# Order of PE's work in a chunk of the convolution part: taps of block 1 and transform 3

## The reference

```python
# layer 0: linear attention
q = elu(to_heads(rope(Wq x + bq)) * scale) + 1;  k = elu(to_heads(rope(Wk x + bk))) + 1;  v = to_heads(Wv x + bv)
out = (q @ (k^T v)) / (q . sum(k) + 1e-6);       layer = Wfc out + bfc
# layer 1: the convolution part
t = einsum('bchw,oc->bohw', x, w_in)             # 384 -> 384
tf = rfft2 of t in 8x8 patches * fft_filter;     t = irfft2(tf)
t = depthwise 3x3 convolution of t with w_dw     # padding SAME
x1, x2 = t[:, :192], t[:, 192:]
layer = einsum('bchw,oc->bohw', gelu(x1) * x2, w_out)
```

## Time and profile before

| | us |
|---|---|
| median of 3 runs | 3960.15 |
| lowest, highest | 3959.14, 3964.23 |
| the profiled execution, its own time | 3959.47 |
| its span, first to last instruction | 3957.6 |
| PE busy | 3490.4 (88%) |
| DVE busy | 3178.0 (80%) |
| POOL busy | 1795.7 (45%) |
| ACT busy | 1629.6 (41%) |

### The profile page before, as it was taken

The page is one execution under the profiler, slowest core; times in us unless marked ns, Lnnn a source line. Parts: engine busy times, 40 slices in busy tenths (PEclk is TensorE's granted clock), DMA queues, the critical chain, the costliest instruction groups (busy, mean ns, idle before and its releaser), DMA issues.

```text
span 3957.6 us, 61233 instructions
## 1 busy us (share of the span) xinstructions
PE 3490.4 (88%) x17808; PEld 3021.8 (76%) x17808; DVE 3178.0 (80%) x4879; ACT 1629.6 (41%) x2781; POOL 1795.7 (45%) x1114
## 2 busy tenths in 40 slices
PE   5988989889898898988989889897889979899798
PEld 4976779767796677966779677896768957699676
DVE  7976979769797697976879768897688976888777
ACT  2423634246342463425633255332553316533164
POOL 2543535435354353553435534454344544444443
PEclk9998989999998999999989899898999989999899
DMA  5113322133212332123321233213332133221322
GB/s 201 64 56 136 119 77 69 64 120 120 89 56 72 121 119 81 57 87 120 112 76 61 88 112 112 89 48 103 109 107 81 48 114 109 96 81 56 128 88 104
DMA packets 186274, 371.18 MB, mean 94 GB/s; under 512 B 7947, under 2 KB 9011, under 8 KB 185779
## 3 DMA queue, kind: packets, MB, share of 16 engines
q1 hardware_dynamic: 186034, 368.26, 27.2%
HBM read 267.56 MB, written 100.66 MB: 93 GB/s over the span
## 4 chain that ended last, share of the span: by engine, by line
issue 33%; PE 30%; POOL 18%; DVE 14%; ACT 3%; DMA 1%; POOLq 1%; DVEq 1%; SPq 0%; ACTq 0%
POOL t L445 9%; POOL x_lo L438 6%; PE bank L1234 5%; PE bank L1200 3%; DVE bank L942 3%; PE bank L1075 3%; PE bank L1076 3%; PE bank L1080 3%; POOL qn L482 3%; PE bank L1207 3%; DVE nrm L850 2%; DVE qt_lo L865 2%; PE bank L1154 2%; DVE xr L878 2%; DVE bn_x L911 2%
## 5 line engine op out<-in xcount | busy, mean ns | idle before, releaser
L445 POOL TENSOR_TENSOR t<-t 128x768 f32<-128x768 f32 x256 | 535.4, 2092 | 726.4 <-DVE t L786 726.4
L1076 PE MATMUL bank<-w_lo,x_hi 128*128 128x384 f32 x2322 | 792.7, 341 | 34.1 <-issue 34.1
L1075 PE MATMUL bank<-w_hi,x_hi 128*128 128x384 f32 x2322 | 789.7, 340 | 4.0 <-ACT x_hi L537 4.0
L438 POOL TENSOR_TENSOR x_lo<-xa,x_hi 128x512 fp32r<-128x512 f32 x363 | 495.9, 1382 | 592.0 <-ACT x_hi L537 592.0
L942 DVE SCALAR_TENSOR_TENSOR bank<-big,wdw,bank 128x512 f32<-128x512 f32 x960 | 685.7, 750 | 94.5 <-PE bank L1234 91.3
L506 POOL TENSOR_TENSOR prod<-prod 128x512 f32<-128x512 f32 x320 | 409.1, 1278 | 489.1 <-ACT prod L629 479.0
L542 ACT ACTIVATE t<-t 128x768 f32<-128x768 f32 x256 | 217.1, 848 | 929.1 <-POOL t L445 929.1
L1080 PE MATMUL bank<-w_hi,x_lo 128*128 128x384 f32 x2322 | 542.3, 342 | 0.5 <-POOL x_lo L438 0.5
L796 DVE SCALAR_TENSOR_TENSOR kt<-t 128x384 f32<-128x384 f32 x256 | 533.6, 2084 | 0.0
L1076 PEld LDWEIGHTS bank<-w_lo,x_hi 128*128 128x128 f32 x2322 | 441.4, 190 | 36.3 <-issue 36.3
L1075 PEld LDWEIGHTS bank<-w_hi,x_hi 128*128 128x128 f32 x2322 | 442.3, 190 | 5.1 <-ACT x_hi L537 4.4
(11 more groups left out here) (127 smaller groups left out, 6800.2 us busy)
## 6 DMA issues: line engine op xcount, KB each, us to landing
xr<-x SPq DMA_DIRECT2D x128, 768.0 KB, 4.7
xa<-x SPq DMA_DIRECT2D x66, 768.0 KB, 6.0
x_scratch<-xr SPq DMA_DIRECT2D x64, 768.0 KB, 3.5
xa<-x_scratch SPq DMA_DIRECT2D x64, 768.0 KB, 5.9
xr<-x_scratch SPq DMA_DIRECT2D x64, 768.0 KB, 4.8
out<-xr SPq DMA_DIRECT2D x64, 768.0 KB, 3.5
big<-x SPq DMA_DIRECT2D x8, 768.0 KB, 10.3
w_raw<-wqkv_t SPq DMA_DIRECT2D x1, 1728.0 KB, 7.3
```

Of the source, the lines that this page charges most:

```text
L438: nc.gpsimd.tensor_tensor(dst, src, hi, ALU.subtract).then_inc(s_lo, 1)
L445: nc.gpsimd.tensor_tensor(a, a, b[:, :, ::-1, :], ALU.add).then_inc(s_add, 1)
L1075: nc.tensor.matmul(dst, hi(k), whi(k), start=first and k == 0, stop=False)
L1076: nc.tensor.matmul(dst, hi(k), wlo(k), start=False, stop=False)
```

## The change

In PE's `part_c`, `taps(c - 1, 1)` is called ahead of `inverse_tile(T + 1, 1)`, and `dft_tile(T + 3, 3)` ahead of `out_block(c - 2, 0)`. The order of the other engines, all waits and all buffers are as before.

```diff
                         t_tile(T + 3, m, par, 3)
                         dft_tile(T + 2, 2)
-                        inverse_tile(T + 1, 1, frees=True)
                     if conv:
                         taps(c - 1, 1)
+                    if tile:
+                        inverse_tile(T + 1, 1, frees=True)
+                    if tile:
+                        dft_tile(T + 3, 3)
                     if prod:
                         out_block(c - 2, 0, last)
                     if tile:
-                        dft_tile(T + 3, 3)
                         inverse_tile(T + 2, 2)
                     if prod:
                         out_block(c - 2, 1, last)
```

## The result

The changed kernel takes 3991.62 us (median of 4 runs, 3991.45 to 3993.68), the kernel before 3959.64 (4 runs): a ratio of 1.0080, 95% interval 1.0063 to 1.0098. It is slower, by 32 us (0.8%) where 22 were forecast. The profiled execution took 3991.45 us, its span (first to last instruction) is 3989.6.

A forecast was written before the change was run, and what follows sets the result against it. The prediction took a loop through PE and DVE, from `rest_wide` over the taps to the residual adds, as the bound. Per image -0.08 + 0.43 + 5 x 0.48 = +2.75 us, over 8 images +22.0, gave 3982 us, range 3967 to 3993.

The forecast's parts named there:

- The main term: Steady chunks: add 0 waits for the later output block 0, costing 0.48 us per chunk.
- The loop and its releaser: Steady chunk: `rest_wide` on DVE releases PE's taps of block 1, which still start 0.25 us later; DVE's wait stays 1.14.
- The slack of 0.82 and the 1.31 placed in front of it: Before add 0: inverse 1 and transform 3 delay output block 0 by 1.31 us; slack takes 0.82, leaving 0.48.
- Not given back: From add 0 to add 1: the 2.21 us chain moves as a whole, so each steady chunk loses 0.48 us.
- What else is late: ACT and POOL: copy of tile 1 comes 1.59 us later, but slacks of 0.81 and over 1 us remain.
- Chunk 1: First tap chunk of an image: taps 0.67 us earlier, inverse 3 gains some 0.08 us; -0.08 us per image.
- rival 3: ACT's delayed copy and casts overrun their 0.81 us slack, moving inverse 3 and output block 2: +37 us, 4020; chance 0.04.
- The clock: Rival: PE's larger hole ahead of the taps lowers the granted clock in 48 chunks: +207 us, some 4190; chance 0.01.

The follow-up runs named there:

- e1: Kernel before with only the first half of the change: taps of block 1 ahead of inverse 1, transform 3 left behind output block 0; 3966.11 us, ratio 1.0022.
- e2: Kernel before with only the second half: transform 3 ahead of output block 0, inverse 1 left ahead of the taps; 3957.61 us, ratio 1.0002.
- e7: Changed kernel with DVE's tap (5, block 0) moved ahead of tap (2, block 1); 3990.80 us, ratio 1.0084.
- e3: Changed kernel with the old order (inverse 1 ahead of the taps) in chunk 1 alone; 3990.71 us, ratio 1.0084.
- e6: Kernel before with DVE's tap (5, block 0) moved ahead of tap (2, block 1); 3927.64 us, ratio 0.9921.
- e4: Changed kernel with PE's steady loop one pass shorter, chunks 6 and 7 unrolled in the changed order; 3992.09 us, ratio 1.0089.
- e5: Changed kernel with PE's steady loop one pass shorter and inverse 1 ahead of the taps in chunk 7 alone; 3983.61 us, ratio 1.0070.

## Why the prediction came out as it did

The measured 3991.62 us lies in the range of 3967 to 3993 us, 1.4 us inside its upper end, and that it does is in part luck. The main term is right and alone leads to the 22 us. The other 10 us come from two costs that the sum did not have, and the width of the range was given for other things: for chunk 1 it had room only for a gain, and for dips only between the parts.

*The loop and its releaser: right.* The taps hang on `rest_wide`. They kept their +0.25 us in the changed kernel, DVE's wait stayed at 1.14, and the page now names the releaser itself.

*The slack of 0.82 and the 1.31 placed in front of it: right, in size too.* Output block 0 came 1.31 us later, add 0 by 0.49 (0.48 forecast), and chunks 2 to 6 took 19.2 us more (18.8 forecast). e1 and e2 show that each group alone stays under the slack; e7 shows that the rest is PE's stretch.

*Not given back: right.* The chain from add 0 to add 1 kept its 2.21 us. *What else is late* was right for the steady chunk: copy of tile 1 +1.59 us, and ACT still waits for PE.

*Chunk 1: wrong in sign*, -0.08 us per image forecast, +0.42 measured. The gain of 0.08 didn't come: inverse 3 of the changed kernel starts at 384.24, in a chunk that began 1.79 us later, against 382.45 before, so nothing was gained. Before, DVE's filter product released it; now ACT's copy of tile 2 does (ending at 384.09), so here, though not in a steady chunk, ACT is late as in rival 3. And I followed POOL's delay only to the reader of its result, the next chunk's `t_tile`, which has slack. I didn't ask which DVE instruction runs beside POOL once POOL is later; 0.5 us relative to the chunk was enough (it starts at 382.73 - 1.79 = 380.94 against 380.41). That instruction is tap (6, block 2), stretched by 0.45 us; e3 takes the stretch away. The Trainium skill ("SBUF — State Buffer", "Terms", its entry on the shared port pair; "GPSIMD Engine Reference", "1. Specifications", its row on the SBUF interfaces) says that DVE and POOL hold one pair of SBUF ports exclusively for a whole instruction, and that DVE meets it with two SBUF inputs. The trace agrees: the tap ends 0.56 us behind POOL's end, while DVE's taps with an operand in PSUM keep their 0.74 to 0.76 us beside POOL's `x_lo` (116 of them in the changed kernel, each beside it for over 0.3 us). The 0.56 us behind POOL's end are less than the 0.76 us that the tap takes alone, so some 0.2 us of it went by beside POOL, and an overlap of 0.07 to 0.08 us (kernel before, e3) costs nothing.

*The clock: the rival's mechanism occurred, where I gave it 0.01.* I compared the enlarged hole (0.97 us by my count, 0.81 in the trace) with the one of 1.31 us in chunk 1, which had left the clock alone, and took one hole for the whole question. The step that failed is that I treated chunk 7 as one of the steady ones. Before the change it has two holes of 0.73 and 0.66 us, because DVE normalises the next input there. Putting the second at 1.33 us made a dip possible, and it costs 2.1 us each time, some 8.4 us in the profiled execution; that it was 4 images and not 0 or 8 hung on the instants at which the clock can change. The row that I set against the rival was also read too widely: the windows behind it end with chunk 7, and the last steps of the part do have a dip (526.80 to 537.04), during a wait of PE of 8.46 us. Taken together the two misses are 4.0 + 7.3 us, chunks 2 to 6 add 0.4 and the other parts of an image gave 1.6 back, and that makes the 10 us between the forecast and the result.

## What to carry to other kernels

Where two engines hand work to and fro, find the releaser of each wait and the slack of each edge of the loop; a group moved ahead of its old place is free until the slack of what it now precedes is used up, and two moves that are free one by one can cost together. Work that is pulled earlier helps nobody if the engine's order isn't what held it: here the wait could be filled from the other side, with a tap that waits for nothing (e6, 0.8% faster). When a list is reordered, look which neighbours now depend on each other: that took back 0.13 of the 0.66 us. And go through the odd iterations one by one (the first, the last, the one with extra work), since over a third of the cost lay there.

## What the runs showed of the hardware

- A DVE instruction with two full-size SBUF operands was held up by a POOL subtraction: 0.76 us alone, 1.15 to 1.23 us when POOL ended 0.59 to 0.67 us behind its start, and then its end came some 0.56 us behind POOL's.
- Two DVE taps of which the second reads what the first writes started 0.79 us apart, two independent ones 0.66 us (e6).
- The granted clock fell within a stretch in which PE was otherwise dense, after two holes of some 0.72 and of 1.23 to 1.33 us with 0.88 us of matmuls between them. It fell in 4, 4, 8 and 7 of 8 images (changed kernel, e7, e3, e4) and in 0 of 8 in e1 with the same holes; with the second hole at 0.56 us in 0 of 8 (e5).
- With those holes it fell exactly where one of the evenly spaced instants of change lay between 0.14 us ahead of the start of the taps and 0.75 us behind it: 23 of 23 images, and 0 of 17 where none lay there.
- Four runs of the changed kernel lie within 2.3 us of each other.
